# Two-digit bf16 one-hots in the routing, four piece buffers in the attention heads, and queries and keys taken by ScalarE

## The reference

```python
x = x + _L0_xattn_ref(_layernorm(x, axis=-1), ctx_1024, ctx_1024, ...)
x = x + _L0_ffn_ref(_layernorm(x, axis=-1), ...)
x = x + _L1_xattn_ref(_layernorm(x, axis=-1), ctx_1024, ...)
x = x + _L1_ffn_ref(_layernorm(x, axis=-1), ...)
x = x + _L2_xattn_ref(_layernorm(x, axis=-1), ctx_1024, ctx_1024, mask_BxSxS2_if1, ...)
x = x + _L2_ffn_ref(_layernorm(x, axis=-1), ...)
x = x + _L3_xattn_ref(_layernorm(x, axis=-1), ctx_1024, ctx_1024, ...)
x = x + _L3_ffn_ref(_layernorm(x, axis=-1), ...)
```

## Time and profile before

| | us |
|---|---|
| median of 3 runs (lowest to highest) | 2483.92 (2481.24 to 2484.52) |
| the profiled execution, its own time | 2488.21 |
| its span | 2486.4 |
| busy: TensorE matmul / weight load | 2020.9 / 1650.8 |
| busy: VectorE / ScalarE / POOL | 1305.6 / 857.8 / 739.1 |
| mean granted clock of TensorE | 0.879 |

### The profile page before, as it was taken

The page is one execution under the profiler, slowest core; times in us unless marked ns, Lnnn a source line. Parts: engine busy times, 40 slices in busy tenths (PEclk is TensorE's granted clock), DMA queues, the critical chain, the costliest instruction groups (busy, mean ns, idle before and its releaser), DMA issues. The chain is left out here.

```text
span 2486.4 us, 41801 instructions
## 1 busy us (share of the span) xinstructions
PE 2020.9 (81%) x13477; PEld 1650.8 (66%) x13477; DVE 1305.6 (53%) x4340; ACT 857.8 (34%) x2004; POOL 739.1 (30%) x928
## 2 busy tenths in 40 slices
PE   6869979983599999999759956996596892898694
PEld 5657756662488989989659944665485671565594
DVE  2542225534488888888320036884546544785423
ACT  4613312421233333333413342445142443355321
POOL 1022100004244444445111022320354745332132
PEclk9959989986699999999869967997697895899697
DMA  2051230002211001110069926335368573641494
GB/s 81 9 207 61 57 116 17 1 1 78 58 31 27 25 26 31 31 27 1 14 236 346 340 100 96 105 93 217 126 157 252 148 137 102 98 101 43 146 313 159
DMA packets 173311, 261.94 MB, mean 105 GB/s; under 512 B 23088, under 2 KB 138800, under 8 KB 169008
## 3 DMA queue, kind: packets, MB, share of 16 engines
q1 hardware_dynamic: 151312, 211.66, 26.0%
q0 software_dynamic: 16704, 45.64, 7.9%
q10 hardware_dynamic: 5088, 1.97, 0.8%
HBM read 181.19 MB, written 37.75 MB: 88 GB/s over the span
## 5 line engine op out<-in xcount | busy, mean ns | idle before, releaser
L1970 PE MATMUL heads_ps_c<-heads_band,heads_sT 128*128 128x129 f32 x3072 | 369.1, 276 | 21.7 <-DVE heads_band L2189 20.7
L1970 PEld LDWEIGHTS heads_ps_c<-heads_band,heads_sT 128*128 128x128 f32 x3072 | 355.2, 192 | 32.1 <-issue 30.2
L2126 POOL TENSOR_SCALAR heads_band<-heads_shifts,heads_taps 128x130 f32<-128x130 f32 x384 | 251.8, 669 | 256.1 <-PE heads_ps_c L1970 251.9
L506 POOL DMA_INDIRECT weights_xg<-xn_rows,token_of x197 | 190.3, 966 | 448.5 <-DVE token_of L686 189.7
L2063 ACT ACTIVATE heads_probs<-heads_mixes,heads_least 128x256 f32<-128x256 f32 x256 | 116.7, 503 | 350.8 <-DVE heads_least L2202 350.8
L2189 DVE SCALAR_TENSOR_TENSOR heads_band<-heads_shifts,heads_taps,heads_band 128x130 f32<-128x130 f32 x768 | 226.3, 350 | 18.7 <-POOL heads_band L2126 14.1
L1672 ACT ACTIVATE heads_probsT<-heads_ps_e 128x512 f32<-128x512 f32 x256 | 146.2, 597 | 150.1 <-PE heads_ps_e L1578 142.8
L1032 PE MATMUL experts_ps_g<-weights_w,experts_xT 128*128 x504 | 136.3, 394 | 2.3 <-ACT experts_xT L1082 1.5
L1171 POOL DMA_INDIRECT combine_yg<-y_rows,slot_of x48 | 45.9, 956 | 300.8 <-POOLq L69 286.8
L1055 PE MATMUL experts_ps_y<-weights_w,experts_hT 128*128 (+1 forms) x486 | 134.1, 385 | 1.1 <-DVE experts_y L1117 1.1
L1554 PE MATMUL heads_ps_m<-heads_stackK,heads_stackQ 96*128 96x256 bf16 x512 | 103.9, 288 | 31.0 <-DVE heads_negmax L1724 21.0
(11 more groups left out here) (386 smaller groups left out, 4373.0 us busy)
## 6 DMA issues: line engine op xcount, KB each, us to landing
experts_w<-in_experts_dram SPq DMA_DIRECT2D x23, 2180.0 KB, 10.4
weights_w<-in_experts_dram SPq DMA_DIRECT2D x16, 1536.0 KB, 17.6
weights_w<-in_experts_dram SPq DMA_DIRECT2D x32, 768.0 KB, 6.4
heads_stackQ<-heads_pieces SPq DMA_DIRECT2D x288, 64.0 KB, 2.7
heads_stackK<-heads_pieces SPq DMA_DIRECT2D x264, 64.0 KB, 2.6
y_rows<-experts_y SPq DMA_DIRECT2D x125, 128.0 KB, 2.0
weights_w<-in_experts_dram SPq DMA_DIRECT2D x8, 1088.0 KB, 15.0
xn_rows<-xn SPq DMA_DIRECT2D x4, 2048.0 KB, 8.5
```

What stands on the lines that cost most here:

```text
L506: pool.indirect_dma_start(self.xg[:, u, :], None, xn_dram, bass.IndirectOffsetOnAxis(ap=tb.token_of[:, j:j + 1], axis=0)).then_inc(self.x_ ...
L1970: last = pe.matmul(out[:, qc * SEQ + k0:qc * SEQ + k1], sT[:, h % 2, kc, qc * P + dq:qc * P + dq + P], band[:, h % 2, dq, w0:w0 + k1 - k0] ...
L2126: last = pool.tensor_scalar(band[:, h % 2, dq, :], shifts[:, 0, :], taps[:, r % 2, h, dq * TAPS:dq * TAPS + 1], None, ALU.mult)
```

## The change

**Routes.** Chunks' one-hots and the numbers compared are bf16 (whole numbers up to 127 and 1, which bf16 holds). The multiplication by the token's number is gone from VectorE; ScalarE writes two products of `tile_hot` into `digits`: with the partition (`tb.column`) and with the number of the token tile. One bf16 matmul for each of the four columns has both digits on its right, 2 NT columns wide. The zero products are gone. At the end the token is the first digit plus 128 times the second. `hot` is written in its own order and read with a stride by TensorE. One gather stands in the route stage in place of three.

```diff
-    COUNT = 3
+    COUNT = 1
...
-        hot = s.sb("hot", [P, E, TILES], BF16)
+        hot = s.sb("hot", [P, TILES, E], BF16)
...
+            for c in range(NK // CH):
+                act.wait_ge(tile_ready, c + 1)
+                if c >= 2:
+                    act.wait_ge(chunk_used, c - 1)
+                act.activation(digits[:, c % 2, :, 0, :], tile_hot[:, c % 2, :, :], ACT.Copy, scale=tb.column[:, 0:1])
+                for n in range(0, CH, K):
+                    last = act.activation(digits[:, c % 2, n:n + K, 1, :], tile_hot[:, c % 2, n:n + K, :], ACT.Copy,
+                                          scale=float((CH * c + n) // K))
+                last.then_inc(chunk_ready, 1)
...
-            pe.matmul(out, ones[:, :], tb.zeros[:, 0:NT], start=True, stop=False, skip_group_check=True)
...
-            flat = hot[:, :, :].rearrange("p e t -> p (e t)")
+            flat = hot[:, :, :].rearrange("p t e -> p e t")
...
+                pe.wait_ge(lane_ready, c + 1)
                 pe.wait_ge(chunk_ready, c + 1)
                 for n in range(CH):
-                    last = pe.matmul(out, lane_hot[:, c % 2, n, :], tile_hot[:, c % 2, n, :], start=False, stop=False,
-                                     skip_group_check=True)
+                    last = pe.matmul(out, lane_hot[:, c % 2, n, :], digits[:, c % 2, n, :, :].rearrange("p d n -> p (d n)"),
+                                     start=(c == n == 0), stop=(c == NK // CH - 1 and n == CH - 1))
                 last.then_inc(chunk_used, 1)
-            pe.matmul(out, ones[:, :], tb.zeros[:, 0:NT], start=False, stop=True, skip_group_check=True)\
-                .then_inc(summed, 1)
...
-                v.tensor_tensor(by_tile(hot[:, :, :]), hot_k[:, 0, :, :], hot_k[:, 1, :, :], ALU.add)\
+                v.tensor_tensor(hot[:, :, :], hot_k[:, 0, :, :], hot_k[:, 1, :, :], ALU.add)\
...
+                v.tensor_tensor(tile_hot[:, c % 2, :, :], tb.iota16[:, 0:NT].unsqueeze(1).to_broadcast([P, CH, NT]),
+                                hi[:, n].unsqueeze(2).to_broadcast([P, CH, NT]), ALU.is_equal).then_inc(tile_ready, 1)
+                v.tensor_tensor(lane_hot[:, c % 2, :, :], tb.iota16[:, :].unsqueeze(1).to_broadcast([P, CH, P]),
+                                lo[:, n].unsqueeze(2).to_broadcast([P, CH, P]), ALU.is_equal).then_inc(lane_ready, 1)
...
+            v.wait_ge(chunk_used, NK // CH)
+            steps.done(v.tensor_copy(tokens[:, 0, :], ps_tok[:, 0:NT]))
+            v.scalar_tensor_tensor(tb.token_of[:, 0:NT], ps_tok[:, NT:2 * NT], float(P), tokens[:, 0, :],
+                                   ALU.mult, ALU.add).then_inc(token_ready, 1)
```

```diff
-        pieces = s.sb("pieces", [P, 2, PIECES, 2, SEQ], BF16)
+        pieces = s.sb("pieces", [P, SLOTS, PIECES, 2, SEQ], BF16)
...
-            if u > 1:
-                engine.wait_ge(stacked[(u - 2) % SLOTS], 16 * stack_dmas * ((u - 2) // SLOTS + 1))
...
+            if u >= SLOTS:
+                engine.wait_ge(stacked[u % SLOTS], 16 * stack_dmas * (u // SLOTS))
...
+            if u > 0:
+                engine.wait_ge(pieces_ready, u)
...
+            def take_query_key(u):
+                p = u % 2
+                act.wait_ge(projected, u + 1)
+                if u == 0:
+                    act.wait_ge(bias_scaled, 1)
+                else:
+                    act.wait_ge(qk_free, u)
+                act.activation(qk[:, 0, :], ps_qk[:, 0:SEQ], ACT.Identity, bias=scaled_bias[:, p:p + 1],
+                               scale=HD ** -0.5)
+                act.activation(qk[:, 1, :], ps_qk[:, SEQ:], ACT.Identity, bias=w[:, WB + DC + p:WB + DC + p + 1])\
+                    .then_inc(qk_taken, 1)
...
             constant_rows(0, SLOTS // 2)
-            for u in range(BY_BOTH):
-                fill_keys(act, u)
+            take_query_key(0)
+            take_query_key(1)
+            fill_keys(act, 0)
+            take_query_key(2)
+            fill_keys(act, 1)
+            take_query_key(3)
             constant_rows(SLOTS // 2, SLOTS)
...
                     act.activation(probsT[:, h, :], ps_e[:, h % 2, :], ACT.Exp).then_inc(exped, 1)
+                    if h == 0 and u + 4 < ROUNDS:
+                        take_query_key(u + 4)
...
+            for u in range(SPLIT_BY_DVE):
+                split(v, u)
+            for u in range(3):
+                place_value(u)
             for h in range(HALF):
                 row_max(0, h)
             split_max(0)
+            for h in range(HALF):
+                row_max(1, h)
             if masking:
                 v.wait_ge(mask_loaded, 32)
                 make_mask(0, 1, mask_ready)
-            for h in range(HALF):
-                row_max(1, h)
...
-                if u + 4 < ROUNDS:
-                    take_query_key(u + 4)
```

```diff
-        pieces = s.sb("pieces", [P, PIECES, 2, SEQ], BF16)
+        pieces = s.sb("pieces", [P, SLOTS, PIECES, 2, SEQ], BF16)
...
-            stack(0, 0)
-            stack(0, 1)
+            stack(0, 0, keys=False)
+            stack(0, 1, keys=False)
...
+            def fill_keys(r):
+                act.wait_ge(pieces_ready, r + 1)
+                for n, (_, a) in enumerate(PRODUCTS):
+                    act.dma_start(stackK[n * HD:(n + 1) * HD, r, :, :], pieces[:, r, a, 1, :]).then_inc(stacked[r], 16)
+
             for r in range(3):
                 place_values(0, r)
+                if r < 2:
+                    fill_keys(r)
...
-                    if not (isinstance(i, int) and u == 0):
-
-                        v.wait_ge(stacked[(r - 1) % SLOTS], 16 * stack_dmas * (i + (r - 1) // SLOTS + 1))
+                    if not (isinstance(i, int) and u < SLOTS):
+                        v.wait_ge(stacked[r], 16 * stack_dmas * i)
```

102 lines of the change are left out of this document (41 added, 61 removed).

## The result

The changed kernel takes 2427.48 us (median of 4 runs, 2422.5 to 2428.19) against 2484.22 for the kernel before in the same comparison: a ratio of 0.9768, 95% interval 0.9754 to 0.9782, 56.7 us less. The forecast was 2431.0. A second comparison, on another chip on which the kernel before took 2509.03, gave 0.9763 (0.9743 to 0.9784).

The account below looks back on a forecast made before the run. It took the kernel as a chain of stages with barriers, each bound by what ends last. Gains of 27.6 + 12.2 + 6.5 + 9.6 + 1 - 2.4 = 54.5 us from the median 2483.9 gave 2429.4, rounded to 2431; range 2417 to 2452.

Parts of the forecast that it names:

- Chunk loops: Route stages' token_of loops: period 1.0 to 1.25 us, loops of 8.3 to 9.9 (K=2) and 4.3 us (K=1).
- One first gather instead of three: Route stages' end: barrier sooner by 0.57 to 3.1 us, 2.5 taken; against it, gathers 1 and 2 issued behind it.
- Last route stage, 5.0: Last route stage and its experts: 4.0 from the loop, 0.6 from `hot`, 0.4 from the gather, 5.0 us gained.
- Route of layer 1, 6.6: Second route stage: 4.0+0.2+2.4 = 6.6 us gained, all counting because its weights start only behind the barrier.
- Heads of layer 1, 12.2: Start of layer 1's heads: four piece buffers end split waits, ScalarE issues keys; 12.2 us gained (11 to 12.5).
- Start of layer 2, 6.5: Start of layer 2's heads: no split waits, ScalarE takes all four, mask asked for earlier; 6.5 us (4 to 7.5).
- Steady rounds of layer 2, 9.6: Layer 2's heads: mask operation falls in a gap between POOL operations, 0.87 x 11 = 9.6 us gained; otherwise 0.
- Layer 3, -1.4: Layer 3's heads: start gains 1 us (0 to 1.8), ScalarE's added operations in steady rounds cost 2.4 (0 to 10).
- the mask behind POOL: Rival 1: layer 2's steady mask operation still waits for POOL, losing the 9.6 us; 2440 us, chance 0.27.
- late gathers in all stages: Rival 2: five route stages each behave like gather 3 of layer 2, 17 us lost; 2448 us, chance 0.12.
- A clock that falls in the steady rounds: Rival 3: ScalarE's takes open gaps in which TensorE falls to 1.2 GHz; slower, 2560 us, chance 0.04.
- loops as long as before: Rival 4: ScalarE's small products cost more than TensorE saves, chunk loops unchanged, 26 us lost; 2457 us, chance 0.05.

Follow-up runs that it names:

- the shift by one exponential: The changed kernel, but ScalarE takes queries and keys behind a round's second exponential, 0.6 us later, instead of the first: ratio 0.9796.

## Why the prediction was right, and where not

The total was 2431 against 2427.5, and the signs of all parts but one were right. That the total is so near is in part luck: the parts of routes and experts brought 22.6 us for a forecast of 27.3, the heads 33.6 for 26.9. By its steps:

- **Chunk loops**: right. 7.6 to 9.4 and 4.0 to 4.3 us, forecast 8.3 to 9.9 and 4.3; the period of 1.06 lies between VectorE's 0.95 and the bound with handovers. ScalarE's 0.93 a chunk was taken as 0.85. Behind the first one-hot product token_of came 7.5, 4.2, 5.8, 5.6 and 3.7 us sooner in the five stages, forecast 7.0, 3.8, 5.65, 5.65 and 3.8. The one-hot's 1.6 was the difference of the two writes; 1.29 is what comes of it. The strided read is hidden, as forecast.
- **"One first gather instead of three"**: the gain at the barrier held. Beside three gathers and the same loops the barrier comes 3.1, 2.5, 2.5, 1.5 and 2.5 us sooner, forecast 2.5 (of which the sums of the stages hold only the 2.4 of layer 1's). What failed is the price of the second gather, which is now issued behind the barrier; it is the prediction's largest error. It was put at 1.0 and 2 us in layer 2's stages and at nothing in the others; TensorE waited 4.54, 7.58, 7.21, 3.32 and 2.98 us in front of the second tile. That both errors cancel is no merit: in layer 2's first group the sum is the same with three gathers, because TensorE then takes its wait later and falls to 0.50 once more.
- **Last route stage, 5.0**: 1.2, and 0.8 of this lies in front of the first one-hot product. The sum counted the loop in full. Against the kernel before, the barrier did come 3.9 us sooner behind that product, the first gate product 1.6 and the last up product only 0.4; the float32 loop put back there cost as little. The 3.0 of the second gather is one part of the loss; another is that the barrier waits until the gather has landed, and with weights in flight (DMA share 1.02 in this loop, 0.00 in layer 1's) a gather that is issued sooner takes longer: the barrier comes 5.1 us behind token_of with the float32 loop and 7.6 with the new one, one gather each. That the weights are the limit is read from these rows, no run takes them away. The prediction said so of the first route stage only (there 3.3 for a forecast of 4.2).
- **Route of layer 1, 6.6**: 7.6, right in mechanism: its weights start behind the barrier.
- **Heads of layer 1, 12.2**: 13.4, with the wait named. That ScalarE's issuing had part in it was wrong, and so were the 1 to 3 us that unit 0 was to land later without it.
- **Start of layer 2, 6.5**: 8.4. The size was near, the cause stood last in the prediction's sentence: taking the mask's order back costs 8.5, and four buffers without the new order bring nothing.
- **Steady rounds of layer 2, 9.6**: 9.5. The step rested on one row and a gap between two POOL operations, and it held to 0.1. Two runs moved the operations and the time followed: 0.42, 0.84, 1.31 us of mask operation give 189.7, 194.2 and 198.5. The mechanism was only read from rows when it was forecast; the Trainium skill, "SBUF — State Buffer", section on the two separate sides, states it: VectorE and GpSimd share a pair of ports as an exclusive lock, which an operation of VectorE needs in a two-port mode or with two SBUF inputs; the one that starts first has it for the whole instruction, the other is fully blocked. The traces agree both ways, 0.14 us short of the full overlap each time: the mask operation is asked for 1.03 before the subtraction's end and takes 0.89 longer, POOL's cast starts 0.35 before the mask operation's end and takes 0.21 longer.
- **Layer 3, -1.4**: +2.1 in the profile. The start gained 2.1 for a forecast of 1, and the steady rounds took 138.4 before and after: ScalarE's takes fit its slack whole (waits for it 21.4 against 22.4).

Of the rivals, the mask behind POOL (2440) is what the shift by one exponential produced in half; late gathers in all stages (2448) did come true as waits, but not as time. A clock that falls in the steady rounds (2560) did not come, ten rounds stood at 1.00, and neither did loops as long as before (2457).

## What to carry to other kernels

In layer 2's first experts' stage a wait of 7.2 us less in front of TensorE was worth nothing, since TensorE came to full speed for good no sooner: look at the granted clock in windows of 1 or 2 us behind a wait before counting it. Before costing an operation of VectorE beside GpSimd, look at what GpSimd does at that moment; a shift of 0.6 us decided 4.5. And a loop 4.3 us shorter was worth 0.4 in a stage that ends with a gather beside a prefetch of weights: look for what lands last.
